# One softmax bound for a query tile instead of one for each head pair, exp waits split by head, and 1/l through ln and exp on ScalarE

## What is computed

```python
qkv = jnp.einsum('bld,ed->ble', x, w_qkv) + b_qkv
q, k, v = jnp.split(qkv, 3, axis=-1)
attn = jax.nn.softmax(jnp.einsum('blhc,bmhc->bhlm', q, k) * SCALE, axis=-1)
heads = jnp.einsum('bhlm,bmhc->blhc', attn, v).reshape(b, l, d)
return jnp.einsum('bld,ed->ble', heads, w_o) + b_o + x
```

## Time and profile before

| | us |
|---|---|
| median of 4 runs | 7303.22 |
| lowest and highest of them | 6951.87, 7396.64 |
| the profiled execution, its own time | 6827.03 |
| its span on core 6, the slowest | 6825.3 |
| spans of the other cores | 6762.2 to 6820.6 |
| PE busy in the span | 4800.6 (70%) |
| ACT busy | 1398.7 (20%) |
| DVE busy | 1645.0 (24%) |

### The profile page before, as it was taken

The page is one execution under the profiler, slowest core; times in us unless marked ns, Lnnn a source line. Parts: engine busy times, 40 slices in busy tenths (PEclk is TensorE's granted clock), DMA queues, the critical chain, the costliest instruction groups (busy, mean ns, idle before and its releaser), DMA issues.

```text
span 6825.3 us, 56603 instructions; the slowest of 8 cores (6762.2 to 6825.3 us)
## 1 busy us (share of the span) xinstructions
PE 4800.6 (70%) x21972; PEld 2084.8 (31%) x21972; DVE 1645.0 (24%) x2492; ACT 1398.7 (20%) x1376; POOL 679.4 (10%) x735
## 2 busy tenths in 40 slices
PE   4755444545454445544599999999957999999998
PEld 2321112111211121112344444444433444444444
DVE  3431213121221222121322222222223222222222
ACT  0005450544145414541000000000001000000000
POOL 0000000000000000000012221122201221222221
PEclk8878785888688768876699999999968999999999
DMA  3120001000100010002277776777744777777775
GB/s 75 37 50 1 2 1 41 10 2 1 38 13 1 2 38 13 1 2 46 20 69 70 71 71 61 70 71 71 71 77 44 74 70 70 71 70 71 70 71 72
DMA packets 924450, 303.72 MB, mean 44 GB/s; under 512 B 899482, under 2 KB 901658, under 8 KB 924194
## 3 DMA queue, kind: packets, MB, share of 16 engines
q0 software_dynamic: 906688, 247.51, 37.4%
q1 hardware_dynamic: 10338, 33.72, 1.4%
q10 hardware_dynamic: 7168, 18.88, 0.7%
HBM read 528.65 MB, written 16.78 MB: 80 GB/s over the span
## 4 chain that ended last, share of the span: by engine, by line
PE 42%; DMA 6%; DVE 3%; issue 1%; ACT 0%; DVEq 0%; ACTq 0%; POOLq 0%; SPq 0%
PE psA L752 15%; PE psB L766 15%; PE psA L797 11%; DMA WS<-W 4%; PE psB L638 1%; DMA out<-OTM 1%; DMA WS<-Ws 1%; DMA YR<-y_scr 1%; PE psA L628 0%; DVE OACC L807 0%; DVE WREP L732 0%; DVE HTMP L777 0%; DVE OTM L837 0%; DVE XL L632 0%; PE psA L727 0%
## 5 line engine op out<-in xcount | busy, mean ns | idle before, releaser
L797 PE MATMUL psA<-HW,WS 128*128 128x512 bf16 x4608 | 1052.8, 389 | 159.7 <-DMA WS<-W 69.1
L752 PE MATMUL psA<-XL,WS 128*128 128x512 bf16 x4608 | 1045.4, 380 | 25.6 <-DVE OACC L807 20.7
L766 PE MATMUL psB<-XL,WS 128*128 128x512 bf16 x4608 | 1041.6, 379 | 0.0
L772 ACT ACTIVATE SILB<-psB 128x1024 bf16<-128x1024 f32 x288 | 295.0, 1024 | 2785.5 <-PE psB L766 2785.5
L418 ACT ACTIVATE PT<-psS_A,NEGG 128x1024 bf16<-128x1024 f32 x512 | 570.6, 1114 | 1228.0 <-PE psS_B L394 1224.7
L388 PE MATMUL psS_A<-QFm,KF 64*128 64x512 bf16 x1024 | 336.7, 411 | 660.8 <-ACT PT L424 647.7
L777 DVE TENSOR_TENSOR HTMP<-psA,SILB 128x1024 bf16<-128x1024 f32 x288 | 352.8, 1225 | 1482.5 <-ACT SILB L772 1482.5
L797 PEld LDWEIGHTS psA<-HW,WS 128*128 128x128 bf16 x4608 | 452.5, 100 | 760.0 <-issue 266.1
L586 POOL DMA_DIRECT2D WS<-W x512 | 448.9, 886 | 2127.2 <-PE psA L752 968.0
L752 PEld LDWEIGHTS psA<-XL,WS 128*128 128x128 bf16 x4608 | 450.5, 98 | 576.4 <-issue 39.2
L766 PEld LDWEIGHTS psB<-XL,WS 128*128 128x128 bf16 x4608 | 450.9, 98 | 543.7
(11 more groups left out here) (128 smaller groups left out, 2729.2 us busy)
## 6 DMA issues: line engine op xcount, KB each, us to landing
WS<-W POOLq DMA_DIRECT2D x512, 256.0 KB, 4.9
WS<-W POOLq DMA_DIRECT2D x128, 512.0 KB, 8.0
XT<-x_kv SPq DMA_DIRECT2D x8, 2048.0 KB
WS<-Ws POOLq DMA_DIRECT2D x64, 256.0 KB, 5.1
XT<-x_own SPq DMA_DIRECT2D x4, 2048.0 KB
Wsh<-wqT POOLq DMA_DIRECT2D x4, 2048.0 KB, 23.5
Wsh<-woT POOLq DMA_DIRECT2D x4, 2048.0 KB, 16.3
y_scr<-YTM ACTq DMA_DIRECT2D x16, 512.0 KB, 2.6
```

What stands on the lines that cost most here:

```text
L752: inst = TE.matmul(psA[:, par, u * 512:(u + 1) * 512], WS1[:, hc % 4, dc, :], XL2[:, dc, u * 512:(u + 1) * 512], start=(dc == 0), stop=(dc ...
L766: inst = TE.matmul(psB[:, par, u * 512:(u + 1) * 512], WS3[:, hc % 4, dc, :], XL2[:, dc, u * 512:(u + 1) * 512], start=(dc == 0), stop=(dc ...
L772: inst = AC.activation(SILB[:, par, :], psB[:, par, :], AF.Silu, bias=0.0, scale=1.0)
L797: inst = TE.matmul(psA[:, par, u * 512:(u + 1) * 512], WS2[:, dcc % 2, hcc, :], HW[:, hcc, u * 512:(u + 1) * 512], start=(hcc == 0), stop= ...
```

## The change

Three parts, all in stage 1b.

First, sampling moves out of the loop over pairs, to the start of a tile. There, 4 chunks are sampled for each of the 8 pairs, 32 steps in a row, the maxima go to a 64-column bf16 `CMS`, and one tail gives one bound for the whole tile, kept in `PRJ[:, 4:5]` (`Gt` and `NEGG` are gone).

Second, the waits of PE for the exps are split: the scores of head A wait for the exp of head A alone, those of head B for that of B, and P*V is reordered to both products of A, then both of B, each behind its own exp.

Third, 1/l at the end of a pair is computed by ACT as exp(-ln l): two Ln of 1x512 from PSUM into a row of `YTM` (as `LNT`), and one Exp of 1x1024 to `LROW`. PE waits for ACT there, and DVE's two reciprocals are gone.

```diff
+                TE.wait_ge(sV.h, sV.v)
+                smBase = sV.v
+                si = 0
                 for p in range(DBG_NPAIR):
-                    TE.wait_ge(sV.h, sV.v)
-                    smBase = sV.v
-                    for idx, cj in enumerate(range(0, NCH, 4)):
-                        if idx >= 2:
-                            TE.wait_ge(sV.h, smBase + idx - 1)
+                    for cj in (0, 8, 16, 24):
+                        if si >= 2:
+                            TE.wait_ge(sV.h, smBase + si - 1)
...
+                negg_v = sV.inc(VE.tensor_copy(PRJ[:, 4:5], psM1[:, 0:1]))
+                AC.wait_ge(sV.h, negg_v)
+                TE.wait_ge(sV.h, negg_v)
+
+                epiV = sV.v
+                shiftSt = sSt.v
+                LNT = YTM[0:1, :].rearrange("p (a b) -> p a b", b=512)
+                for p in range(DBG_NPAIR):
                     tBase = sT.v
                     aBase = sA.v
                     for k in range(17):
                         if k < 16:
                             if k >= 1:
-                                TE.wait_ge(sA.h, aBase + 2 * k)
+                                TE.wait_ge(sA.h, aBase + 2 * k - 1)
...
+                            if k >= 1:
+                                TE.wait_ge(sA.h, aBase + 2 * k)
...
-                            TE.wait_ge(sA.h, aBase + 2 * kk + 2)
+                            TE.wait_ge(sA.h, aBase + 2 * kk + 1)
...
+                            TE.wait_ge(sA.h, aBase + 2 * kk + 2)
+                            for u in range(2):
+                                j = 2 * kk + u
...
-                    VE.wait_ge(sT.h, sT.v)
+                    AC.wait_ge(sT.h, sT.v)
+                    AC.activation(LNT[:, 0, :], psPV_A[64:65, :], AF.Ln,
+                                  bias=0.0, scale=1.0)
+                    AC.activation(LNT[:, 1, :], psPV_B[64:65, :], AF.Ln,
+                                  bias=0.0, scale=1.0)
+                    AC.drain()
...
-                        VE.reciprocal(LROW[:, 0, :], psPV_A[64:65, :])
-                        sV.inc(VE.reciprocal(LROW[:, 1, :], psPV_B[64:65, :]))
-                    TE.wait_ge(sV.h, sV.v)
+                        inst = AC.activation(LROW[:, :, :], LNT[:, :, :], AF.Exp,
+                                             bias=0.0, scale=-1.0)
+                    sA.inc(inst)
+                    TE.wait_ge(sA.h, sA.v)
```

More of the change, by code:

```diff
@@ L345, in emit_phase1 @@
                                   tile_position=(0, 0))
-                        inst = TE.matmul(psS_B[:, idx % 2, :],
+                        inst = TE.matmul(psS_B[:, si % 2, :],
                                          KF[64:128, p, 128 * cj:128 * (cj + 1)],
@@ L351, in emit_phase1 @@
                         VE.wait_ge(sT.h, sT.v)
-                        sampA = psS_A[:, idx % 2, :].rearrange(
+                        sampA = psS_A[:, si % 2, :].rearrange(
                             "p (a b) -> p a b", b=4)[:, :, 0]
-                        sampB = psS_B[:, idx % 2, :].rearrange(
+                        sampB = psS_B[:, si % 2, :].rearrange(
                             "p (a b) -> p a b", b=4)[:, :, 0]
-                        VE.reduce_max(CMS[:, 2 * idx:2 * idx + 1], sampA, axis=AX.X)
@@ L367, in emit_phase1 @@
[L367 to L379, removed]
+                        with nc.allow_low_precision(
+                                reason="sampled maxes for the softmax bound; the "
+                                       "+20 margin absorbs bf16 rounding"):
+                            VE.reduce_max(CMS[:, 2 * si:2 * si + 1], sampA, axis=AX.X)
+                            inst = VE.reduce_max(CMS[:, 2 * si + 1:2 * si + 2], sampB,
+                                                 axis=AX.X)
@@ new lines, in emit_phase1 @@
+                        sV.inc(inst)
+                        si += 1
+                VE.drain()
+                VE.reduce_max(CM1[:], CMS[:], axis=AX.X)
+                sV.inc(VE.drain())
+                TE.wait_ge(sV.h, sV.v)
+                sT.inc(TE.transpose(psM1[0:1, 0:128], CM1[:], identf[:]))
+                VE.wait_ge(sT.h, sT.v)
+                VE.reduce_max(PRJ[0:1, 0:1], psM1[0:1, 0:128], axis=AX.X)
+                VE.drain()
+                VE.tensor_scalar(PRJ[0:1, 1:2], PRJ[0:1, 0:1], SCALE, 20.0,
+                                 ALU.mult, ALU.add)
@@ new lines, in emit_phase1 @@
+                VE.drain()
+                VE.tensor_scalar(PRJ[0:1, 2:3], PRJ[0:1, 1:2], -1.0, None, ALU.mult)
+                sV.inc(VE.drain())
+                TE.wait_ge(sV.h, sV.v)
+                sT.inc(TE.matmul(psM1[:, 0:1], ones32[:], PRJ[0:1, 2:3],
+                                 start=True, stop=True))
+                VE.wait_ge(sT.h, sT.v)
+                negg_v = sV.inc(VE.tensor_copy(PRJ[:, 4:5], psM1[:, 0:1]))
+                AC.wait_ge(sV.h, negg_v)
+                TE.wait_ge(sV.h, negg_v)
@@ L420, in emit_phase1 @@
                                 psS_A.rearrange("p a b -> p (a b)"),
-                                AF.Exp, bias=NEGG[:], scale=SCALE))
+                                AF.Exp, bias=PRJ[:, 4:5], scale=SCALE))
                             AC.wait_ge(sT.h,
```

19 lines of the change are left out of this document (3 added, 16 removed).

## The result

The changed kernel takes 6173.1 us (median of 7 runs, 6162.99 to 6620.04) against 6900.08 us before (10 runs, 6829.14 to 7396.64). The ratio is 0.904, with a 95% interval of 0.899 to 0.909: 9.6% faster. In some executions, of either kernel, the cores of one half of the chip run up to several hundred us longer at a lower clock, and the ratio leaves such runs out, among them all four that the prediction took its median from.

What follows compares the result with a forecast made beforehand. No engine was taken as the bound: ACT and PE wait for each other in turn, and gaps separate pairs. Terms -307 - 388 - 19 + 68 = -646 us, taken from the median 7303, gave 6657 us; range 6130 to 6820.

Steps and rivals of the forecast that it cites:

- The base: Whole kernel: the profiled execution's 476 us below the median was carried over, so the saving was taken from 7303, not 6827.
- The loop: Attention loop in stage 1b: split waits cut the period from 2.96 to 2.22 us, saving 307 us over 32 pairs.
- The chain of 3.43 us: Attention loop: time from the start of B's exp to A's exp two iterations later, through scores and four P*V.
- The change of shape: PE's switch from P*V back to scores in the loop, taken as 0.10 us.
- The pair's end: Gaps between pairs: 22.21 us shrink to 8.37, 388 us over 28 gaps; 19 more after the tiles' last pairs.
- Sampling: Start of each tile: 24 more sampling steps of 0.71 us, 17.1 us a tile, adding 68 us over four tiles.
- The clock: Start of each pair's loop: two iterations still run at 1.2 GHz, as before, adding 1.4 to 1.6 us.
- The clock high over a pair's boundary: Rival: the clock stays at 2.4 GHz between pairs, saving 70 us more, 6587 us; chance 0.11.
- Table loads: Rival at the pair's end: ACT loads tables at each ln, two a pair, costing 82 us, 6739 us; chance 0.04.
- An unchanged loop: Rival: the loop period stays at 2.96 us, only gaps and sampling count, -339 us, 6964 us; chance 0.06.
- The low clock throughout: Rival: PE stuck at 1.2 GHz, 3.6 us an iteration; no change, chance 0.02, or with drains 7521 us, chance 0.02.
- The sum as a whole: All terms of attention together: -307 - 388 - 19 + 68 = -646 us, which takes 6827 to 6181.

Runs made afterwards that it cites:

- e5: The changed kernel with P*V of A moved between the scores of A and the scores of B; 7134.72 us.
- e7: The changed kernel with P*V of A between the scores, next pair's first scores ahead of the 1/l spreading matmuls, and tmpB's DMA issued by SP; 7275.32 us, ratio 1.004.
- e9: The changed kernel with P*V of A between the scores of A and B from a pair's fifth iteration on, the first four unchanged; 6135.12 us, ratio 0.899.

## Why the prediction was right in its steps and wrong in its number

**The base.** The step that failed is this one: "Since attention takes the same steps in both, I carry the difference over: 7303 - 646 = 6657 us." The 476 us between the profiled execution and the median were not a fixed part of the kernel's time but belonged to those four runs. Of six more runs of the kernel before, five lie between 6829 and 6849, at the profiled 6827. The hint was there: the profiled execution was below all four, and they spread over 445 us, far more than the sum could depend on. Set against 6900, the median of ten runs, 6657 is a change of 3.5%, where 9.6% was measured. The range, 6130 to 6820, did hold 6173, because its lower end was counted from 6827.

**The loop** (-307). The chain of 3.43 us gave 2.22; measured are 2.235, a pair 37.24 for 37.2, and the pairs together lose 312. Alone the waits saved 331 us, for 307 plus the 14 of the last P*V, which the prediction had put into the gaps.

**The change of shape**, taken as 0.10 between bounds of 0 and 0.41: it is 0.10.

**The pair's end** (-388 and -19). 8.10 us for 8.37, and the 28 gaps together lose 396. On its own the ln saved 142 us. The estimate between 4 and 1024 elements was right to 0.02 us (0.59 for 0.61).

**Sampling** (+68). 21.64 us for 22.8 a tile. The step was taken as 0.71, from eight steps with a slow first one; in a long row it is 0.68.

**The clock.** Two low-clock iterations in the pair shown, as forecast, and the fall inside the gap, as in the kernel before. The reason given for them was thin: that the clock "rises today after two iterations with less PE work in them than the new ones have". e5 has more PE work still, and inside its loops it never rises. What lets it rise is open. The prediction did not see two things that come before each rise here, the late scores of the two heads side by side and the four P*V in a row; it weighed the loss of the pairing at the high clock only. That the two iterations came out is in part luck.

**The rivals.** The clock high over a pair's boundary: no, it falls in the gap. Table loads: none. An unchanged loop: no. The low clock throughout: not in this kernel, but in e5 and e7.

The sum as a whole: 646 forecast, 666 until the end of attention, of which the stage after gave back 11.

## What to carry to other kernels

Where one engine makes what another eats, in two halves, release each half on its own, and work out the period as the chain over two turns, with everything that stands behind the released instruction in its engine's order. Before matmuls are moved into a waiting place, look at what the clock does in the iterations before it has risen: an order that is better at 2.4 GHz (2.17 for 2.235) can keep it at 1.2 GHz, and then costs 12% here (6906 for 6163, lowest runs). And add a sum of differences to the runs that the profile belongs to, not to a median from which the profiled run stands out.

## What the runs showed of the hardware

- A PE that is busy without a pause (49.00 of 49.00 us, by the modelled ends of its matmuls) can stay at 1.2 GHz. Couples of 64-row scores and of P*V with 65 output columns in strict turns never raised the clock inside a loop of e5; six P*V in a row at the end of its pairs did, for a moment (1.00 from 638 to 640). In the changed kernel the same eight matmuls an iteration, with four P*V in a row and then the scores of two row groups side by side, raised it behind 745.7.
- The same order, entered at 2.4 GHz, is run at 2.4 GHz (1.00 from 748 to 763.5 in e9).
- Two row groups ran side by side without being asked to, where the waits between them were already met: starts 745.70 and 745.71, although a wait instruction stands between them in PE's order.
- A stage that no edit touches took 3669 to 3703 us in the five executions compared here.
